# Half of the even states' products moved from the vector engine to ACT and PE in a bidirectional state-space scan

## What is computed

```python
dA  = jnp.exp(dt[..., None] * A)
dBu = dt[..., None] * Bm[:, :, None, :] * xs[..., None]
def combine(c1, c2):
    a1, b1 = c1
    a2, b2 = c2
    return (a1 * a2, a2 * b1 + b2)
_, hs = jax.lax.associative_scan(combine, (dA, dBu), axis=1)
y = jnp.einsum('blds,bls->bld', hs, Cm) + xs * Dvec
```

## Time and profile before

| what | value |
|---|---|
| median of 3 runs | 1490.27 us (1488.96 to 1495.98) |
| span of the profiled execution | 1493.7 us |
| PE busy | 1262.7 us, 85% |
| DVE busy | 1200.8 us, 80% |
| ACT busy | 898.4 us, 60% |
| POOL busy | 836.4 us, 56% |
| DVE scans (L1364), 256 | 570.3 us busy |
| DVE products (L1352), 144 | 177.0 us busy |

### The profile page before, as it was taken

One profiled execution on the slowest core, in us unless ns is written; L12 is line 12 of the kernel. 1 busy time (PEld: TensorE's weight loads), 2 busy tenths in 40 slices (PEclk: granted clock), 3 DMA queues, 4 the chain that ended last, 5 costly groups with the idle time before them and its releaser, 6 DMA issues. The chain is left out here.

```text
span 1493.7 us, 17449 instructions
## 1 busy us (share of the span) xinstructions
PE 1262.7 (85%) x4573; PEld 641.1 (43%) x4573; DVE 1200.8 (80%) x1388; ACT 898.4 (60%) x1247; POOL 836.4 (56%) x450
## 2 busy tenths in 40 slices
PE   3609888898998988988888989889898998888868
PEld 1307344344546434433444634434354733434343
DVE  2695799998796689999688679999779479999920
ACT  1626766766555766767464676676574676676612
POOL 3022388788152378778235258878517238878815
PEclk8859899999989889999999979999999988999979
DMA  2000112222030112222021012222103011322203
GB/s 77 14 0 2 46 71 84 85 92 77 16 113 15 31 57 86 85 86 97 17 77 66 4 58 79 91 85 86 56 1 114 16 37 65 98 85 84 85 1 127
DMA packets 30506, 92.00 MB, mean 62 GB/s; under 512 B 4790, under 2 KB 8764, under 8 KB 30428
## 3 DMA queue, kind: packets, MB, share of 16 engines
q1 hardware_dynamic: 30428, 91.10, 18.0%
HBM read 88.34 MB, written 2.75 MB: 61 GB/s over the span
## 5 line engine op out<-in xcount | busy, mean ns | idle before, releaser
L664 POOL TENSOR_TENSOR work<-expo,ring 128x1024 f32<-128x1024 f32 x128 | 300.1, 2365 | 164.4 <-DVE expo L1364 162.3
L664 POOL TENSOR_TENSOR ring<-ring 128x1024 f32<-128x1024 f32 x128 | 300.2, 2367 | 26.7 <-DVE ring L1364 26.7
L1364 DVE TENSOR_TENSOR_SCAN ring<-ring,ps 128x1024 f32<-128x1024 f32 x128 | 284.7, 2263 | 6.9 <-PE ps L1786 6.9
L1364 DVE TENSOR_TENSOR_SCAN expo<-ring,ps 128x1024 f32<-128x1024 f32 x128 | 285.6, 2270 | 0.0
L1822 PE MATMUL ps<-ring,ident 128*128 128x512 f32 x512 | 260.4, 615 | 25.5 <-POOL ring L664 18.7
L1822 PE MATMUL ps<-work,ident 128*128 128x512 f32 x512 | 241.1, 593 | 0.0
L953 ACT ACTIVATE ring<-dt_f,decay 128x1024 f32<-128x1024 f32 x128 | 147.0, 1148 | 118.9 <-DVE expo L1364 80.7
L719 ACT ACTIVATE b_dtx_tok<-dtx_tok,b_tok 128x256 f32<-128x256 f32 x448 | 189.2, 493 | 0.0
L1786 PE MATMUL ps<-ident,b_dtx_tok 128*128 128x128 f32 x896 | 121.8, 279 | 43.9 <-DVE expo L1364 40.1
L1786 PEld LDWEIGHTS ps<-ident,b_dtx_tok 128*128 128x128 f32 x896 | 96.8, 141 | 134.0 <-issue 69.2
L1822 PEld LDWEIGHTS ps<-ring,ident 128*128 128x128 f32 x512 | 83.7, 189 | 159.7 <-POOL ring L664 116.6
(11 more groups left out here) (280 smaller groups left out, 2075.6 us busy)
## 6 DMA issues: line engine op xcount, KB each, us to landing
ring<-c_rows SPq DMA_DIRECT2D x128, 512.0 KB, 3.6
b_dtx_tok<-comb_rows SPq DMA_DIRECT2D x16, 512.0 KB, 4.0
dtx_tok<-comb_rows SPq DMA_DIRECT2D x16, 512.0 KB, 4.7
x_c<-in_x SPq DMA_DIRECT2D x4, 512.0 KB, 3.3
out<-xs_f SPq DMA_DIRECT2D x4, 512.0 KB, 2.6
w<-in_L_ffn_w SPq DMA_DIRECT2D x2, 512.0 KB
ring<-in_L_attn_f_in_proj_w SPq DMA_DIRECT2D x1, 256.0 KB
ring<-in_L_attn_b_in_proj_w SPq DMA_DIRECT2D x1, 256.0 KB
```

Of the source, the lines that this page charges most:

```text
L664: pool.tensor_tensor(hc[odd][:, k, :], hs[odd][:, k, :], c_all[:, odd, :], ALU.mult).then_inc(hc_ready, 1)
L1364: v.tensor_tensor_scan(hs[odd][:, k, order], dA[:, k, order], dbu[:, order], 0.0, ALU.mult, ALU.add).then_inc(scan_ready, 1)
```

## The change

From pair 2 on (6 of 8 pairs in each direction, 48 in all), the last 512 of the 1024 tokens of the even state are made the odd state's way. ACT scales four tiles of `dtx_tok` by the even state's B (`weigh_even`, into `b_even_tok`, which reuses the storage of `prob_t`). PE transposes them, four per block, into the upper bank of the PSUM tile (`turn_even`). Its `spread` then makes only the lower 512 columns, and DVE's products cover only those. An even scan now waits for both. The order on PE changes with it, and pair 1, which stays as it was, is taken out of the loops.

```diff
+        BY_TOKEN = range(TILES // 2, TILES)
+        b_even_tok = prob_t[:, 0, :, :].rearrange("p a c -> p (a c)").rearrange("p (a c) -> p a c", c=BLOCKS * P)
...
+                def weigh_even(r, tiles):
+
+                    act.wait_ge(dt_ready, (b + 1) * DIRS * BLOCKS)
+                    act.wait_ge(even_turned, 2 * (mixed + r - 2))
+                    for i in tiles:
+                        last = copy(b_even_tok[:, i - BY_TOKEN[0], :], dtx_tok[:, i, :],
+                                    scale=b_tok[:, d, i, ds(2 * r, 1)])
+                    if TILES - 1 in tiles:
+                        last.then_inc(even_weighted, 1)
...
                     decay_of(2 * r + 1, 0)
+                    if not last:
+                        weigh_even(r + 1, BY_TOKEN[:2])
                     decay_of(2 * r + 1, 1)
+                    if not last:
+                        weigh_even(r + 1, BY_TOKEN[2:])
...
-                    v.tensor_tensor(state_in[1 - turn if k == 0 else turn][:, :], dtx[d][k], state_in[turn][:, :],
-                                    ALU.mult).then_inc(dbu_ready, 1)
+                    v.tensor_tensor(state_in[1 - turn if k == 0 else turn][:, columns], dtx[d][k][:, columns],
+                                    state_in[turn][:, columns], ALU.mult).then_inc(dbu_ready, 1)
...
+                scan(b, d, 2 * r, 0, turn, k, (dbu_ready, 2 * (spreads + r + 1) + k + 1),
+                     also=(even_turned, 2 * (mixed + r - 1)))
...
+            def turn_even(b, d, r, turn, k):
+
+                base = b * UNITS + d * BLOCKS * D_STATE
+                pe.wait_ge(scan_ready, base + 4 * r - k)
+                pe.wait_ge(even_weighted, (b * DIRS + d) * (PAIRS - 2) + r - 1)
+                to = state_in[1 - turn if k == 0 else turn]
+                for i in BY_TOKEN:
+                    last = tr(to[:, i * P:(i + 1) * P], b_even_tok[:, i - BY_TOKEN[0], k * P:(k + 1) * P],
+                              ident[:, :])
+                last.then_inc(even_turned, 1)
...
-                    spread(b, d, 2 * r + 2, 1 - turn)
+                    spread(b, d, 2 * r + 2, 1 - turn, parts=[0])
+                    add(b, d, r, 0, [1], [0])
+                    turn_even(b, d, r + 1, 1 - turn, 1)
+                    turn_even(b, d, r + 1, 1 - turn, 0)
+                    add(b, d, r, 0, [1], [1])
                 else:
                     then()
-                add(b, d, r, 0, [1])
+                    add(b, d, r, 0, [1])
```

More of the change, by code:

```diff
@@ L311, in hybrid_block @@
         turned_back = sem("turned_back")
+        even_weighted = sem("even_weighted")
+        even_turned = sem("even_turned")
         c_rows_stored = sem("c_rows_stored")
@@ L965, in weigh_by_b @@
                         last.then_inc(weighted, 1)
+                mixed = e * (PAIRS - 2)
+                def weigh_even(r, tiles):
[6 more added lines that the diff above has]
+                        last.then_inc(even_weighted, 1)
                 def to_tokens(k):
@@ L1001, in direction, with pair @@
                     decay_of(1, 1)
-                with act.Fori(2 if d == 0 else 1, PAIRS) as r:
+                def pair(r, last=False):
                     decay_of(2 * r, 0)
@@ L1007, in direction @@
                     decay_of(2 * r + 1, 0)
+                    if not last:
+                        weigh_even(r + 1, BY_TOKEN[:2])
                     decay_of(2 * r + 1, 1)
+                    if not last:
+                        weigh_even(r + 1, BY_TOKEN[2:])
+                with act.Fori(2 if d == 0 else 1, PAIRS - 1) as r:
+                    pair(r)
+                pair(PAIRS - 1, last=True)
             def act_image(b, m=None):
@@ L1337, in dtx_forward, with products @@
                 v.tensor_tensor(dtx[0][k], dt[0][k], xs[0][k], ALU.mult).then_inc(dtx_ready, 1)
-            def products(b, d, s, n, turn, first=False):
+            def products(b, d, s, n, turn, first=False, columns=slice(0, N)):
                 base = b * UNITS + d * BLOCKS * D_STATE
@@ L1350, in products, with scan @@
                         dve.wait_ge((dtx_ready, dtx_b_ready)[d], b * BLOCKS + k + 1)
-                    v.tensor_tensor(state_in[1 - turn if k == 0 else turn][:, :], dtx[d][k], state_in[turn][:, :],
-                                    ALU.mult).then_inc(dbu_ready, 1)
-            def scan(b, d, s, odd, turn, k, made, first=False):
+                    v.tensor_tensor(state_in[1 - turn if k == 0 else turn][:, columns], dtx[d][k][:, columns],
+                                    state_in[turn][:, columns], ALU.mult).then_inc(dbu_ready, 1)
+            def scan(b, d, s, odd, turn, k, made, first=False, also=None):
                 base = b * UNITS + d * BLOCKS * D_STATE
@@ L1360, in scan @@
                 dve.wait_ge(*made)
+                if also is not None:
+                    dve.wait_ge(*also)
                 dve.wait_ge(hc_ready, base if first else base + unit - 3)
@@ L1370, in scan_product, with scan_mixed @@
                 scan(b, d, s, odd, turn, k, (dbu_ready, 2 * (spreads + n) + k + 1), first)
+            def scan_mixed(b, d, r, turn, k):
+                spreads = (b * DIRS + d) * SPREADS
+                mixed = (b * DIRS + d) * (PAIRS - 2)
+                scan(b, d, 2 * r, 0, turn, k, (dbu_ready, 2 * (spreads + r + 1) + k + 1),
+                     also=(even_turned, 2 * (mixed + r - 1)))
             def scan_turned(b, d, r, turn, k):
@@ L1384, in apply_gate, with state_pair @@
                 v.tensor_tensor(gate[:, d, k, :], gate[:, d, k, :], ps[2 * k][:, :], ALU.mult).then_inc(gated, 1)
-            def state_pair(b, d, r, turn):
-                products(b, d, 2 * r, r + 1, turn)
+            def state_pair(b, d, r, turn, mixed=True):
+                products(b, d, 2 * r, r + 1, turn, columns=slice(0, BY_TOKEN[0] * P) if mixed else slice(0, N))
                 for k in range(BLOCKS):
-                    scan_product(b, d, 2 * r, 0, r + 1, turn, k)
+                    (scan_mixed(b, d, r, turn, k) if mixed
+                     else scan_product(b, d, 2 * r, 0, r + 1, turn, k))
                 for k in range(BLOCKS):
@@ L1393, in later_states @@
             def later_states(b, d):
+                state_pair(b, d, 1, d, mixed=False)
                 with dve.Fori(1, PAIRS // 2) as j:
-                    state_pair(b, d, 2 * j - 1, d)
                     state_pair(b, d, 2 * j, 1 - d)
-                state_pair(b, d, PAIRS - 1, d)
+                    state_pair(b, d, 2 * j + 1, d)
             def mamba(b, following):
@@ L1767, in skip_term, with spread @@
                        start=True, stop=False)
-            def spread(b, d, s, turn, first=False):
+            def spread(b, d, s, turn, first=False, parts=range(HALVES)):
                 base = b * UNITS + d * BLOCKS * D_STATE
                 pe.wait_ge(scan_ready, base if first and d == 0 else base + 2 * s - 1)
-                for h in range(HALVES):
+                for h in parts:
                     last = mm(halves(state_in[turn])[h], pick[:, ds(s, 1), :].rearrange("p o m -> p (o m)"),
```

2 lines of the change are left out of this document (added).

## The result

The changed kernel takes 1437.67 us, the median of 4 runs (1434.79 to 1439.81), against 1489.62 for the kernel before in the same rounds: a ratio of 0.9639, with a 95% interval of 0.9615 to 0.9662. Forecast were 1441 and a range of 1434 to 1466. Two later series of the change gave 0.9651 (0.9628 to 0.9673) and 0.9651 (0.9615 to 0.9687).

A forecast was written before the change was run, and what follows sets the result against it. DVE, without a gap in the scans, was taken as the bound: 48 x 1.07 = 51.4 us less 2 for the start gives 49.4 off 1493.7, 1444.3; with the median 0.23% below the span, 1441 us, range 1434 to 1466.

The forecast's parts named there:

- DVE's products: Two products per mixed pair go from 1024 to 512 columns on DVE, saving 1.07 us a pair, 51.4 us over 48.
- The bounds of 0.97 and 1.23: Lower and upper ends, in us a pair, for what DVE saves by halving the columns of its two products.
- The added wait on the even scan: On DVE, the even scan's extra wait costs nothing by itself if what it waits for is there.
- PE's cover: PE's work in a mixed pair comes to 9.71 us, under DVE's 10.18, with 0.47 us to spare.
- The first rival: PE becomes the bound in mixed pairs: nine waits at 0.10 us each, pairs of 10.6, about 1459 us; chance 20%.
- The hand-off: PE's even transposes reach DVE's even scan in time: PE arrives 0.1 us early, with 0.5 us of lateness covered behind.
- 0.73 is left: ACT's 3.46 us idle a pair, less 1.07 for the shorter pair and 1.66 for four copies, leaves 0.73 us.
- POOL, SP: POOL gets no new work, its wait shrinks from 1.91 to some 0.84 us; SP's loads of C's rows hold nothing up.
- Start: POOL's 2.13 us split makes each of four forward directions start late by 0.5 us, 2 us in all; ends 0 and 8.5.
- The third rival: PE's clock falls to 1.2 GHz in the scans, 9.2 us more per affected pair, 1514 us; chance 8%.
- Nothing changes: Pairs stay near 11.25 us because PE, ACT or the transpose timing loses what DVE gains; 1490 us within 7; chance 6%.

## Why the prediction was right

*DVE's products.* 1.07 us a pair from a price per column between two of DVE's own operations: measured 11.25 - 10.18 = 1.07. The bounds of 0.97 and 1.23 were not needed. The added wait on the even scan cost nothing, as assumed.

*PE's cover.* 9.71 us of work in 10.18, so 0.47 to spare: doubling the transposes made the pair 10.59, which is 9.71 + 0.88. That sum is also what PE takes without a pause where DVE's products are nearly gone, 9.71. The first rival failed on this: of the nine waits that could each have cost 0.10, the pair shows few, and none that reached a scan. PE's 61.88 of 62 us busy would have been misread as a bound; its starts were not.

*The hand-off.* Forecast with 0.1 us and behind it 0.5 to spare; 0.26 and 0.4 to 0.5 measured. Shifting it by 0.86 us cost 0.1 a pair, so 0.76 us were there, and the step held. (The first scan of two lasts 2.28 us by itself, not the 2.25 of the working, which moves no term by more than 0.03.)

*ACT.* The verdict, that ACT delays nothing, held, and its working did not. The step "0.73 is left" took ACT's idle time as its spare; by starts it was 1.22, and doubling the copies cost 0.37 a pair where 0.93 was expected on that ground. It did not matter to the time because both are above zero.

*POOL, SP.* POOL's wait per pair was to shrink to 0.84 us: it reads 0.83. C's rows still land 3.6 us after issue.

*Start.* The term of 2 us was too large: one pair of a forward direction takes 10.42 to 10.45, some 0.25 us more than the rest, about 1 us over the four. I had put it on POOL and on PE's backlog; the split on POOL alone makes it, as moving it showed.

*The clock.* As before, it is low ahead of a forward direction's scans and rises with them; with 24 transposes in a pair where there were 16, it stays at 1.00, 2.4 GHz (windows after, columns as above; the last row is the run with all eight tiles by token, 32 transposes in a pair):

```profile
186.00:190.00 4.00, 4.00 (x7) 1.50 (x8) 3.14 (x2) 4.00 (x8) 4.00 (x2) 0.54 0.00 0
202.00:212.00 10.00, 9.90 (x42) 5.57 (x41) 9.93 (x7) 9.21 (x17) 10.00 (x5) 1.00 0.22 68
222.00:260.00 38.00, 37.93 (x154) 20.09 (x152) 37.72 (x23) 34.77 (x59) 34.34 (x16) 1.00 0.30 106
295.00:345.00 50.00, 50.00 (x233) 30.06 (x232) 42.37 (x20) 50.00 (x96) 44.61 (x20) 1.00 0.29 105
```

The third rival is out. The rule of the Trainium skill (TensorE: Matmul & The Clock Gate, "Part 4: PE-mode transpose") by which transposes leave the full clock unengaged did no harm here, where products stand between them. "Nothing changes" is out with the pairs.

The forecast was 3 us above the median, and the scans don't account for it: they gave 49.2 us of the 49.4. That these two agree so well is partly luck. The 48 steps into a pair with half products gave 50.2 us, since the start cost about 1 us and not 2; the other steps from pair to pair, which the change doesn't touch, took 1.0 us more in this profile, and the two repeats come to 47.6 and 47.5. So the 3 us lie outside the scans, where executions differ by several us, and no run here tells whether any of it is the change's.

## What to carry to other kernels

When one engine is without a gap, a piece of its work can be split by columns between it and the engines that idle beside it; more of it isn't always better, since the next engine fills up (here half gave 0.964, all of it 0.972). A share between wasn't run, so half isn't shown to be the best: by the sums above, five tiles of eight would leave DVE 10.18 - 2 x 128 x 1.05 ns = 9.91 us in a pair and PE 9.71 + 2 x 0.109 - 0.22/4 = 9.87, an estimate without the hand-off. What a neighbour can take is read from its starts in a stretch where it never waits: busy time overstates a pipelined PE, and idle time understates the spare of ACT. A moved piece needs a place in the other queue where it is done before it is wanted; here DVE's remaining products covered the hand-off.

## What the runs showed that was not expected

ACT's operations overlap by about 0.1 us when it doesn't wait: a 1024-column exponential lasts 1.14 to 1.15 us but the next operation starts 1.04 later, and a 256-column copy lasts 0.49 and takes 0.40. The Trainium skill (ScalarE: Activation LUTs, "What ACT_TABLE_LOAD costs") puts the overlap of back-to-back ACTIVATEs at some 93 ns. These runs agree, with 0.09 us for the copy and 0.10 for the exponential. The working of the prediction had left that tail out. So 1.2 us of room in a pair showed up as 0.7 us of waits. And PE, read as 99.8% busy in the scans, still took another 0.46 us of work per pair free of charge.
